# Layer 1's attention interleaved into the expert stage, with a state matrix for the lower half of the retention

## The reference

```
q, k, v  = xh @ Wq, xh @ Wk, xh @ Wv          # 8 heads of 16, per head
scores   = (q . k) * gamma_h ** (n - m)  for m <= n, else 0
ret      = scores @ v, then normalised per head (mean 0, variance 1), * gn_w + gn_b
attn     = (silu(x @ W1) + ret) @ W2
probs    = softmax(x @ Wr + br); an expert is kept while the sum of the
           sorted probabilities is under 0.8 (the first always)
ffn      = sum over 8 experts of gate_e * (relu(x @ W1_e + b1_e) @ W2_e + b2_e)
x        = x + attn(layernorm(x)) + ffn(layernorm(x))      # hidden width 512
```

## Time and profile before

| | |
|---|---|
| runs, median | 770.96 us |
| profiled execution, first to last instruction (its own time inside the program) | 765.3 us |
| busy PE / DVE / ACT / POOL | 703.9 / 546.6 / 419.5 / 327.7 us |
| experts, 409 to 759.6 us | PE busy 349.25 of 350.6 |
| layer 1's DVE operations of 256 columns, mean | 0.407 to 0.432 us |
| the reciprocal of 16, the copy of 272 | 0.248, 0.440 us |
| q/k times decay, 512 columns | 0.682 us |
| ACT of 256 columns: copies, q_odd, zT | 0.376 to 0.384, 0.500, 0.477 us |
| ACT normalising one tile of 128, root of 16 | 0.486, 0.304 us |
| POOL: gn_w, gate added, one half of v_ring, ones | 0.740, 0.790, 0.314, 0.516 us |
| POOL: centring or low part of a weight; 256 wide order | 1.28; 0.731 us |
| table loads of ACT between 290 and 425 us | 4 of 1.283 us |
| DMA | 66.51 MB, 87 GB/s mean |

### The profile page before, as it was taken

One profiled execution on the slowest core, in us unless ns is written; L12 is line 12 of the kernel. 1 busy time (PEld: TensorE's weight loads), 2 busy tenths in 40 slices (PEclk: granted clock), 3 DMA queues, 4 the chain that ended last, 5 costly groups with the idle time before them and its releaser, 6 DMA issues.

```text
span 765.3 us, 17690 instructions
## 1 busy us (share of the span) xinstructions
PE 703.9 (92%) x6133; PEld 526.3 (69%) x6133; DVE 546.6 (71%) x1053; ACT 419.5 (55%) x802; POOL 327.7 (43%) x433
## 2 busy tenths in 40 slices
PE   5787788998899978989898999999999999999997
PEld 4643445556755547757666888888888888888885
DVE  6878997885678866779886766666665666666665
ACT  5645665676477678677664444444444444444442
POOL 3765643783758860147694631212122221222222
PEclk9999999999999999999999999999999999999999
DMA  6984655431134420012114611112121212111100
GB/s 188 261 239 137 179 133 201 167 95 49 51 120 129 142 85 1 12 33 61 54 43 117 156 52 56 56 41 69 41 69 41 69 41 59 50 52 58 41 15 14
DMA packets 63795, 66.51 MB, mean 87 GB/s; under 512 B 6512, under 2 KB 41840, under 8 KB 63728
## 3 DMA queue, kind: packets, MB, share of 16 engines
q1 hardware_dynamic: 62128, 63.23, 27.7%
q0 software_dynamic: 1024, 2.12, 1.0%
q10 hardware_dynamic: 576, 0.27, 0.1%
HBM read 47.46 MB, written 17.99 MB: 86 GB/s over the span
## 4 chain that ended last, share of the span: by engine, by line
PE 75%; DVE 9%; issue 5%; ACT 4%; DMA 3%; POOL 2%; SPq 1%; ACTq 0%; POOLq 0%; DVEq 0%
PE ps L1763 25%; PE ps L1992 22%; PE ps L1876 3%; DVE m L1241 3%; PE ps L1683 3%; PE ps L1587 3%; PE ps L1796 2%; PE ps L1831 2%; PE ps L1593 2%; PE ps L1597 2%; PE ps L1897 1%; DMA qk_parts<-qk_p 1%; PE ps L1601 1%; PE ps L1688 1%; PE ps L1580 1%
## 5 line engine op out<-in xcount | busy, mean ns | idle before, releaser
L963 ACT ACTIVATE f_h<-ps 128x512 fp32r<-128x512 f32 x256 | 153.3, 599 | 197.6 <-PE ps L1763 197.6
L1463 DVE SCALAR_TENSOR_TENSOR f_l<-ps,f_h 128x512 fp32r<-128x512 f32 x256 | 175.9, 691 | 112.5 <-ACT f_h L963 111.3
L1763 PE MATMUL ps<-x_hl,w_h 128*128 (+1 forms) x512 | 200.3, 391 | 0.0
L783 POOL TENSOR_TENSOR acc<-acc,yt 128x512 f32<-128x512 f32 x55 | 70.9, 1289 | 249.8 <-DVE yt L1501 249.8
L877 ACT ACTIVATE probs<-ps 128x1536 f32<-128x1536 f32 x64 | 92.8, 1450 | 34.4 <-PE ps L1606 33.8
L1763 PEld LDWEIGHTS ps<-x_hl,w_h 128*128 128x128 f32 x512 | 96.1, 188 | 19.6
L682 POOL TENSOR_SCALAR_AFFINE_SELECT probs<-probs 128x512 f32<-128x512 f32 x128 | 78.4, 637 | 59.8 <-ACT probs L877 59.5
L1992 PE MATMUL ps<-f_l,w_h 128*128 128x512 f32 x256 | 99.8, 390 | 1.3 <-DVE f_l L1463 1.3
L1992 PE MATMUL ps<-f_h,w_h 128*128 128x512 f32 x256 | 99.7, 390 | 0.0
L1763 PE MATMUL ps<-x_hl,w_l 128*128 (+1 forms) x256 | 99.6, 389 | 0.0
L1992 PE MATMUL ps<-f_h,w_l 128*128 128x512 f32 x256 | 99.6, 389 | 0.0
(11 more groups left out here) (225 smaller groups left out, 1328.2 us busy)
## 6 DMA issues: line engine op xcount, KB each, us to landing
gate_b<-gate_rows SPq DMA_DIRECT2D x64, 256.0 KB, 3.3
qk_parts<-qk_p SPq DMA_DIRECT2D x16, 512.0 KB, 3.8
k_st<-qk_parts SPq DMA_DIRECT2D x64, 96.0 KB
q_st<-qk_parts SPq DMA_DIRECT2D x64, 96.0 KB
y_tok<-zero SPq DMA_DIRECT2D x8, 512.0 KB, 2.9
w_raw<-in_w_e SPq DMA_DIRECT2D x16, 256.0 KB, 2.7
x_rows<-xn_rows SPq DMA_DIRECT2D x8, 260.0 KB, 3.2
w_up<-in_w_up SPq DMA_DIRECT2D x8, 256.0 KB, 2.7
```

The source lines that it names most:

```text
L783: nc.gpsimd.tensor_tensor(acc[:, :], acc[:, :], yt[:, e % 2, :], ALU.add).then_inc(summed, 1)
L963: nc.scalar.activation(r32(f_h[:, m % 4, :]), ps[:, m % 4, :], ACT.Relu).then_inc(f_hi, 1)
L1463: nc.vector.scalar_tensor_tensor(out=r32(f_l[:, m % 4, :]), in0=ps[:, m % 4, :], scalar=0.0, in1=f_h[:, m % 4, :], op0=ALU.max, op1=ALU.su ...
L1763: last = nc.tensor.matmul(dst, r32(lhs[i]), r32(rhs[j]), start=(k == 0), stop=(k == 2))
```

## The change

Layer 1's first two stages are gone as stages. Units are numbered through all blocks (0 to 255), and a window of 16 units carries one sequence: `between(n)` puts PE's work of retention and projections between `hidden` and `output` of a unit, `when` says in which unit each later step falls, and the `unit(n)` of ACT, DVE and POOL puts theirs in the same order. Before unit 0 stands a short prologue with the projections of sequences 0 to 2. Scores need only the two diagonal blocks: what the first 128 tokens give to the last 128 goes by a state, the 128x128 product of the decayed token-major keys and v (`sum_state`; `put_state` keeps each head's own block), which the queries multiply in `weigh1`. For it the token-major product is 128 columns wider for the first tile. Gates are worked out per block of 512 tokens; the first three experts of block 0 are gated later, by POOL. `hidden` has three banks, `output` one. The constants and first weights of layer 1 are loaded at group 60 of layer 0, through a ring of four buffers, and all blocks are written out.

```diff
-UNITS = E * FC
-AHEAD = 3
+UNITS = NB * E * FC
+EXPERTS = NB * E
+WINDOW = 16
+RAWS = 4
+LATER = 3
+RETURNS = 60
+KPROJ1 = P + PROJ1
...
+        def ps_t1(b): return ps[:, b if b < 2 else 0 if b == 2 else 4, 0:S]
+        def ps_qk1(b): return ps[:, 2 + b if b < 2 else 5, :]
+        def bank_p1(b): return 4 if b in (0, 2) else 6
+        def ps_state(b): return ps[:, 4 if b == 0 else 7, 0:P]
+        ps_o1 = ps[:, 4, 0:S]
+        ps_at1 = ps[:, 4, 0:S]
+        ps_r1 = ps[:, 5, 0:S]
+        ps_zt = ps[:, 5, S:2 * S]
+        ps_sum = ps[:, 6, :]
+        def ps_gates(j): return ps[0:TPB * E, 5 if j else 4, S:S + P]
+
+        def ffn(n): return n // (E * FC), n // FC, n % FC
+        def when(w, name):
+
+            late = {"values_by_scores": 6, "turn_z": 7, "put_z": 10, "put_o": 9, "turn_o": 10, "project": 11, "heads": 13,
+                    "add": 14, "squares": 14, "root": 15, "divide": 16}
+            usual = {"values_by_scores": 9, "turn_z": 8, "put_z": 11, "put_o": 12, "turn_o": 12, "project": 13, "heads": 15,
+                     "add": 16, "squares": 17, "root": 18, "divide": 19}
+            return w * WINDOW + (late if w == B - 1 else usual)[name]
+        def inputs_of(b): return [x_hl[:, b // 2 % 3, i, b % 2 * S:(b % 2 + 1) * S] for i in range(2)]
...
+            def load_weights(e):
+
+                load_raw(e, 0)
+                if e >= 1:
+                    sp.wait_ge(centred, e)
+                sp.dma_start(w1_first[:, :], a["w1_first"][:, ds(e, 1), :].rearrange("p o f -> p (o f)")).then_inc(first_in, 16)
+                load_raw(e, 1)
+            def load_second_layer():
+
+                sp.wait_ge(y_put, E)
+                sp.wait_ge(consts_ready, 6)
+                sp.wait_ge(x1_half, 4)
+                for dst, name in ((gam[:, :, :], "gam"), (gam_k[:, :], "gam_k"), (odd_rows[:, :], "odd_rows"), (own_head[:, :], "own_head"),
+                                  (not_after[:, :, :], "not_after")):
+                    sp.dma_start(dst, a[name]).then_inc(late_in, 16)
+                load_weights(0)
+                if num(g) == RETURNS:
+                    load_second_layer()
...
+            centre(0)
+            low_w1(0)
+            centre(1)
+            values(0)
+            add_bias(0)
+            less_max(0)
+            put_ones(0)
+            low_w1(1)
+            weigh_probs(0)
+            values(1)
+            order_probs(0)
+            def unit(n):
+
+                w, p = divmod(n, WINDOW)
+                if n < E * FC:
+                    for e in range(2, E):
+                        if n == max(FC * e - 10, 0):
+                            centre(e)
+                        if n == FC * e - 6:
+                            low_w1(e)
+                if n == 2:
+                    keep_experts(0)
+                if n == 13:
+                    for g in range(LATER):
+                        gate_later(g)
+                        add_expert(g)
+                if n % FC == 2 and n // FC > LATER:
+                    add_expert(n // FC - 1)
+                if p == 6 and 2 <= w + 1 < B:
+                    values(w + 1)
+                    if when(b, "divide") + 1 == n:
+                        weigh_heads(b)
+                if w % 2 == 0 and 1 <= j < NB:
+                    if p == 12:
+                        add_bias(j)
+                    if p == 14:
+                        less_max(j)
+                j = (w + 1) // 2
+                if w % 2 == 1 and j < NB:
+                    if p == 1:
+                        weigh_probs(j)
+                    if p == 4:
+                        order_probs(j)
+                    if p == 8:
+                        put_ones(j)
+                    if p == 10:
+                        keep_experts(j)
...
+                act.wait_ge(h_mm, n + 1)
+                if n >= 4:
+                    act.wait_ge(y_mm, n - 3)
+                nc.scalar.activation(r32(f_h[:, n % 4, :]), ps[:, n % 3, :], ACT.Relu).then_inc(f_hi, 1)
...
+            deviation1(2, LATE)
+            put_gate(0)
+            high_w1(1)
             halve(0)
+            high_x(2)
+            put_gate(1)
+            halve(1)
+            normalise(3, 1)
+            put_gate(2)
+            exponentials(0)
+            def unit(n):
+
+                w, p = divmod(n, WINDOW)
+                hidden_unit(n)
+                for e in range(1, E):
+                    if e >= 2 and n == max(FC * e - 7, 0):
+                        high_w1(e)
+                    if n == FC * e - 4:
+                        high_w2(e)
+                if p == 15 and w % 2 == 0 and w // 2 + 1 < NB:
+                    exponentials(w // 2 + 1)
+                for b in falls("root", n):
+                    root_of(b)
+                if p == 5 and w + 4 < B:
+                    normalise(w + 4, w % 2)
+                if p == 7 and w + 3 < B:
+                    high_x(w + 3)
+                if p == 9 and w + 2 < B:
+                    halve(w + 2)
+                if p == 10 and w + 3 < B:
+                    put_gate(w + 3)
+                for b in falls("put_z", n):
+                    if b >= 1:
+                        put_z(b - 1)
+                for b in falls("put_o", n):
+                    put_o(b)
+                for b in falls("heads", n):
+                    put_heads(b)
...
-                        split_layer1(w1_p, w1_raw[:, 2 * P:])
+                        split_layer1(w1_p, w1_raw[:, P:])
...
+                nc.vector.tensor_tensor(k_tok[:, b % 2, :], ps[:, bank_p1(b), 0:P], gam_k[:, :], ALU.mult).then_inc(k_put, 1)
+                nc.vector.tensor_copy(v1[:, b % 4, :, :], ps[:, bank_p1(b):bank_p1(b) + 2, P:2 * P + E]).then_inc(v1_put, 1)
+                nc.vector.tensor_tensor(states[:, b % 3, :], ps_state(b), own_head[:, :], ALU.mult).then_inc(state_put, 1)
+                dve.wait_ge(s1_done, b + 1)
+                if b >= 1:
+                    dve.wait_ge(pv1_done, b)
+                nc.vector.tensor_tensor(sc[:, h, :, :], ps[:, 4 + h, :].rearrange("p (k t) -> p k t", t=P),
+                                        upto[:, :].unsqueeze(1).broadcast_to([P, 4, P]), ALU.mult).then_inc(masked, 1)
...
                 dve.wait_ge(f_hi, n + 1)
-                nc.vector.scalar_tensor_tensor(out=r32(f_l[:, m % 4, :]), in0=ps[:, m % 4, :], scalar=0.0, in1=f_h[:, m % 4, :],
+                if n >= 4:
+                    dve.wait_ge(y_mm, n - 3)
+                nc.vector.scalar_tensor_tensor(out=r32(f_l[:, n % 4, :]), in0=ps[:, n % 3, :], scalar=0.0, in1=f_h[:, n % 4, :],
                                                op0=ALU.max, op1=ALU.subtract).then_inc(f_lo, 1)
...
+            def gate_expert(g):
+                j, e = divmod(g, E)
+                i = j * (E - 1) + e - 1
+                dve.wait_ge(y_mm, (g + 1) * FC)
                 if e == 0:
-                    if known_block(j) != 0:
-                        dve.wait_ge(acc_turned, j)
...
+                    if j >= 2:
+                        dve.wait_ge(acc_turned, j - 1)
+                elif i >= 3:
+                    dve.wait_ge(summed, i - 2)
+                dst = yt[:, i % 3, :] if e else acc[:, j % 2, :]
+                if g < LATER:
+                    nc.vector.tensor_scalar(dst, ps[:, 3, :], b2[:, e:e + 1], None, ALU.add).then_inc(yv, 1)
+                else:
+                    dve.wait_ge(gate_in[g % 4], g // 4 * 16 + 16)
+                    nc.vector.scalar_tensor_tensor(out=dst, in0=ps[:, 3, :], scalar=b2[:, e:e + 1],
+                                                   in1=gate_b[:, g % 4, :], op0=ALU.add, op1=ALU.mult).then_inc(yv, 1)
...
+            put_qk(0)
+            put_values(0)
+            put_qk(1)
+            put_state(0)
+            low_x(2)
+            shift_of(2, LATE)
+            put_values(1)
+            gate_max(0)
+            low_w2(0)
+            put_values(2)
+            put_state(1)
+            gate_sum(0)
+            compare(0)
+            def unit(n):
+
+                w, p = divmod(n, WINDOW)
+                split_unit(n)
+                if n % FC == 1 and n >= FC:
+                    gate_expert(n // FC - 1)
+                if n == 2:
+                    sum_up_to(0)
+                if 3 <= p < 7:
+                    mask_scores(w, p - 3)
+                if p == 7 and w + 2 < B:
+                    put_qk(w + 2)
+                if p == 8 and w + 3 < B:
+                    low_x(w + 3)
+                if p == 11 and w + 3 < B:
+                    put_values(w + 3)
+                if p == 15 and w + 2 < B:
+                    put_state(w + 2)
+                if p == 15 and w % 2 == 0 and w >= 2:
+                    finish(w // 2 - 1)
+                for b in falls("add", n):
+                    if b >= 1:
+                        add_retention(b - 1)
+                for b in falls("squares", n):
+                    square_sums(b)
+                for b in falls("divide", n):
```

(107 more changed lines are left out.)

842 lines of the change are left out of this document (343 added, 499 removed).

## The result

The changed kernel takes 781.48 us (median of 4 runs, 780.9 to 783.84), the kernel before 770.83 beside it: ratio 1.014 [1.0114, 1.0165]. It is slower by 1.4%, and the interval leaves 1 out. On another chip the comparison gave 1.0135 [1.0103, 1.0167]. Forecast were 753 us and "faster" at 0.85; 781 lies outside the range of 740 to 768 as well.

A forecast was written before the change was run, and what follows sets the result against it. Expert stage taken as PE-bound, the 121 us ahead as bound by latency and alternation. Start 303.5 + units 348.2 + sums 3.1 + PE's extra 86 + end 6.3 = 747.1 us span; with 5.7 carried over, 753 us, range 740 to 768.

The forecast's parts named there:

- Start: Layer 0's end to first units: layer 0 ends about 1.2 us later, projections start at 289.2, steady work from 303.5.
- Waits and cover: Early weight work lies under the first 28 units; uncovered up to 1 us per expert, 7; cover is the four-slot ring.
- Unit time: Expert stage: six 512-column matmuls per unit, 1.36 us, 256 units 348.2 us, plus 3.1 for block sums; nothing changes.
- PE's extra: Retention and projections among expert units: 5.7 us more PE time per 16-unit window, 86 us in all after deductions.
- the bounds of 77 to 97: PE's extra in total: 77 us for plain streams alone, 97 with 0.26 for each of six insertions per window.
- Rival 3: Single output bank: PE waits 0.4 us for each of 64 gatings, 25.6 us, giving 779 us; chance 0.09, above 773.3.
- Rival 2: Late evacuation: a table load or busy DVE holds PE 0.9 us per window, 15 us, giving 768; chance 0.2.
- rival 1: Cheap insertions: PE's extra near 77 us and start near 300.5, giving 741 us; chance 0.18 for 736 to 745.
- Rival 4: Change falls short: PE's extra takes 97 us, start is 306, with some stalls of 4 us, giving 770.5; chance 0.06.
- the engines keep up: Steady windows of 27.7 us: DVE 81% busy, ACT 63%, POOL a third; none is the bound by sum.
- the table loads: ACT in the expert stage: about 37 loads of 1.28 us, hidden by two units of lead, cost nothing; otherwise 48 us.
- the end: Closing chain: the last add goes from DVE, 0.69 us, to POOL, 1.29, so 5.7 us becomes 6.3.

The follow-up runs named there:

- experiment 12: Changed kernel rerun, 779.94 us; then with 416 bytes more unused space so all operands share one offset, 776.01 us, ratio 1.0078 to the kernel before.
- Experiment 2: Changed kernel with block 0's gate transfer and four broadcasts issued behind expert 4's weights instead of expert 3's: 789.82 us, ratio 1.0057 to the kernel before.
- Experiment 7: Changed kernel; layer 1 loads behind last row maximum, gates behind expert 5's row, fifth gate one expert later, late gating over units 15-17: 783.16 us, ratio 0.9976.
- 13: Kernel of Experiment 7 plus a 32-byte shift and two alternating weight-row buffers, each row requested one expert earlier: 782.29 us, ratio 0.9986 to the kernel before.
- 14: Kernel of 13 with all operands at one offset and block 0's gate broadcasts two and two behind the weights of experts 4 and 5: 761.34 us, ratio 0.9889.
- 10: Kernel before with W1 and hidden parts moved to 256, W2 at 160 bytes behind a multiple of 512: 790.67 us, ratio 1.0101 to the kernel before.
- experiment 9: Kernel before with two unread transposes behind every second unit: 817.04 us, ratio 1.0435; separately, with extra DVE and ACT copies instead: 784.25 us, ratio 1.0009.

## Why the prediction was wrong

**Start (wrong by 4.3 us).** "That transfer went at about 272.5; behind 3.4 us of issues it goes at 276 and lands near 278, ... layer 0 ends about 1.2 later." The mechanism is the right one, the size is not. Layer 0 was 2.4 us later already ahead of this transfer (277.83 against 275.47 in the rows above). No run shows that the change causes this: on the chip of experiment 12 the same exponential starts at 276.30 in the changed kernel and at 276.86 in the kernel before with 64 bytes apart. With these 2.4 us the forecast issue at 276 comes at 278.4, and 278.62 was measured. The landing was mis-sized: the scores follow the issue by 3.25 us and not 2. With that the last exponential loses 2.7 us instead of 1.2. Another 0.4 comes behind it, under the half clock.

**Waits and cover (wrong by about 12 us with the clock, the largest part).** "The early weight work lies under the first 28 units; uncovered it would be up to a microsecond per expert, 7 ... its cover is the four-slot ring." The work itself was sized rightly. What failed was its cover: I counted the engines' time and not SP's queue, in which the gate transfers of block 0 stand between the weights of experts 3 and 4, wait there for ACT, and then put a megabyte ahead of a row for which GpSimd, ACT, DVE and PE wait in one chain. The four-slot ring covers the raw weights; `w_first` has a single slot and no cover. Asking of `keep_gates(0)` what is queued behind it on SP would have shown it. Experiment 2 moved the burst by one expert, and the wait of 6.5 us went to the next row. Experiment 7 put it behind the row of expert 5 and spread GpSimd's late gating: the first two windows fell to 64.1 us. Two buffers for the row (13) gave nothing more, broadcasts two and two (14) brought 63.0. They are still 6.6 us above two steady ones. That the burst delays the row is measured (9 us from issue to landing against 2.7); how much of experiment 7's gain is its place and how much the spread gating stays open.

**The clock.** No step had a price for it. The earlier trace rows show 0.96 in the retention stage, and I took the clock as 1.00 from the start of the units. The pause of 7 us was followed by matmuls 0.42 apart, so it cost more than its length: some 4 of the 14.3 us that windows 0 and 1 take beyond two steady ones. In experiment 14, where the waits are short, the half clock goes too.

**Unit time, "Nothing of this changes" (wrong by 9 us).** Order, duration and count of the 512-column matmuls are the same, but not the place of their operands in the SBUF. Experiments 10 and 12 show it from both sides: pulling them apart costs the kernel before 5.5 ns per matmul, putting them together gives the changed one 4.2 of its 5.8 back. The remaining 1.6 ns come with the insertions. Nothing in the trace of before could show the first part, since all its operands stand alike.

**PE's extra (mis-sized by about 6 us).** The sum has 5.7 per window; a steady window of 28.6 less 96 spacings of 232.5 ns and the 0.2 for the sums leaves 6.1. Measured from the last regular matmul ahead to the second behind, less their spacing, scores cost 1.30 (1.10 of their own, and 0.1 each on entering and leaving) where 1.03 was taken; the recorded work stays near the estimate, the entries and exits were left out. The total, about 92, is within the bounds of 77 to 97. The upper bound was added up wrongly: sixteen times 5.1 and six times 0.26, less 5.5, is 101.

**Rivals.** Rival 3 gave 779 us, almost what was measured, by a mechanism that is not there: PE never waits for the gating. A right number is no proof. Rival 2 is refuted by the same list of waits, rival 1 by the size of the insertions, which came out above the forecast and not below. Rival 4 names three causes that are there, a larger extra, a late start and some stalls, but the stalls are three times its 4 us, and the spacing is missing.

**What held.** In the steady stretch the engines keep up (DVE 71%, ACT 53%, under the forecast 81 and 63), the table loads cost nothing that the waits show, and the late evacuation never stalls PE. Repaired in its queue order and layout, the same idea gives 757.7 us of span, 10.6 over the forecast: waits and half clock ahead of the third scores 3.0, the spacing of 228.3 ns 2.5, the insertions 5.7 and the end 0.9, less 1.5 for the projections, which start at 287.7 and not at 289.2.

## What to carry to other kernels

When work is interleaved to fill an engine, go through the DMA-issuing queue as through an engine: for each issue that waits, list the issues behind it and their readers, and for each large transfer, what lands after it. A load with a single buffer and a chain of engines behind it goes ahead of any burst. After a change of buffers, compare the spacing of the commonest matmul before looking for waits: 64 bytes between buffers cost here as much as a stall of some 5 to 8 us.

## What the runs showed of the hardware that was not expected

- 512-column fp32r matmuls with reloaded weights follow each other by 226.7 ns when weights and moving operands start at the same offset to a multiple of 512 bytes (160 or 192 all, two kernels), by 232.2 when they are 64 or 96 bytes apart (two kernels), by 230.8 and 232.5 in the changed kernel at 128 and 96. It is not the distance within one matmul alone: in the changed kernel the hidden products have weights and moving operand both at 256, only the output products are apart, and yet the three matmuls of a hidden product follow each other by 232.2 and 234.5 ns. Which distances are free was not searched, nor why.
- Short matmuls put between them raise the spacing of the rest to 231.1 (128 pairs, experiment 9), though no engine waits. In the changed kernel with its operands together it is back at 226.7 from the eighth matmul behind an insertion.
- A 256 KB row asked for right behind four broadcasts of 256 KB landed after 9 us. The profile page's median for the raw weights, of the same size, is 3.2. The four broadcasts themselves took 3.9, 5.8, 7.5 and 8.6.
- The kernel before takes 770 us on two chips and 784 to 785 on three others, 1.8% more. The difference lies in layer 0: from the start of layer 1's projections to the end it is the same within 2 us. Its cause was not looked for.
